# Local attention and FFN layers on one core: four hand-written orders of steps are replaced, and the next stage's first steps move among the last tiles

## The reference, cut to what matters

```python
for i in range(DEPTH):                               # DEPTH = 6
    x = attn_layer(shift_tokens(x), Wqkv[i], q_scale[i], k_scale[i], Wo[i]) + x
    x = ffn_layer(shift_tokens(x), ln_g[i], ln_b[i], W1[i], b1[i], W2[i], b2[i]) + x

# attn_layer: 16 heads of 64, window 32
q, k, v = jnp.split(x @ Wqkv, 3, -1)                 # 128 -> 3 x 1024
q = l2norm(q) * qs;  k = l2norm(k) * ksc             # then a rotary table on each
sim = q_window @ k_two_windows * 8, masked;  attn = softmax(sim, -1)
out = (attn @ v_two_windows) @ Wo
# ffn_layer: layer norm, 128 -> 2 x 341, a * gelu(gate), 341 -> 128
```

## Time and profile before

| what | value |
|---|---|
| runs | 2055.22, 2067.45, 2062.59 us, median 2062.59 |
| span of the profiled execution | 2060.2 us |
| PE busy | 1889.6 us, 92% of the span |
| DVE, ACT, POOL busy | 1444.6, 1395.0, 1448.5 us (70%, 68%, 70%) |
| mean granted TensorE clock | 0.967 |

### The profile page before, as it was taken

How to read it: one execution, slowest core, us unless ns; L and a number is a source line. 1 busy time by engine, 2 the same in 40 slices (tenths; PEclk the granted TensorE clock), 3 DMA queues, 4 the chain that set the end, 5 groups by cost and what they waited for, 6 DMA issues and landing times. The chain is left out here.

```text
span 2060.2 us, 77645 instructions
## 1 busy us (share of the span) xinstructions
PE 1889.6 (92%) x32069; PEld 1309.8 (64%) x32069; DVE 1444.6 (70%) x2609; ACT 1395.0 (68%) x2772; POOL 1448.5 (70%) x1839
## 2 busy tenths in 40 slices
PE   4648999999999999999999999999999999879959
PEld 3526666666666666666666666666666676656648
DVE  2357787678776877786778777877687778445546
ACT  1147877777777677877787778777777777534425
POOL 1158887787788778887888788878887888412334
PEclk9769999999999999999999999999999999979969
DMA  2012131111311111211113111121111111030012
GB/s 97 0 22 58 52 97 46 33 53 55 97 46 48 47 46 58 88 46 46 46 49 97 46 46 46 31 82 31 33 31 31 36 33 31 13 94 1 22 32 71
DMA packets 67087, 99.84 MB, mean 48 GB/s; under 512 B 15367, under 2 KB 51608, under 8 KB 65970
## 3 DMA queue, kind: packets, MB, share of 16 engines
q1 hardware_dynamic: 65234, 91.72, 15.4%
q0 software_dynamic: 1504, 3.17, 0.5%
HBM read 44.50 MB, written 21.45 MB: 32 GB/s over the span
## 5 line engine op out<-in xcount | busy, mean ns | idle before, releaser
L1284 PE MATMUL b_bank_proj<-layer_weights,b_stream_t 128*128 128x512 f32 x1152 | 587.1, 611 | 33.9 <-DVE b_plain_moved L1080 17.9
L1080 DVE TENSOR_TENSOR b_plain_moved<-b_bank_proj,b_rope 128x1024 f32<-128x1024 f32 x384 | 463.9, 1219 | 190.0 <-ACT b_squares L912 136.7
L820 POOL TENSOR_TENSOR b_rotated<-b_plain_moved 128x1024 f32<-128x1024 f32 x192 | 453.7, 2363 | 22.4 <-DVE b_plain_moved L1080 18.6
L835 POOL TENSOR_TENSOR b_rotated<-b_rotated,b_inv_norm 128x1024 f32<-128x1024 f32 x192 | 365.4, 1903 | 15.6
L943 ACT ACTIVATE b_k_t<-b_bank_shared 64x512 f32<-64x512 f32 x384 | 226.5, 590 | 121.9 <-PE b_bank_shared L1292 119.3
L912 ACT ACTIVATE b_squares<-b_bank_proj 128x512 f32<-128x512 f32 x384 | 229.2, 597 | 114.3 <-PE b_bank_proj L1284 109.9
L1284 PEld LDWEIGHTS b_bank_proj<-layer_weights,b_stream_t 128*128 128x128 f32 x1152 | 186.3, 191 | 135.9 <-issue 45.7
L840 POOL TENSOR_TENSOR b_probs<-b_probs,b_inv_sum 128x512 f32<-128x512 f32 x192 | 200.6, 1045 | 84.3 <-DVE b_inv_sum L1101 82.8
L1292 PE MATMUL b_bank_shared<-const_tables,b_rotated 128*128 128x128 f32 x1536 | 233.1, 277 | 17.4 <-POOL b_rotated L835 17.3
L934 ACT ACTIVATE b_q_t<-b_bank_shared 64x512 f32<-64x512 f32 x384 | 225.7, 588 | 34.3 <-PE b_bank_shared L1292 31.5
L1292 PEld LDWEIGHTS b_bank_shared<-const_tables,b_rotated 128*128 128x128 f32 x1536 | 177.9, 141 | 108.3 <-issue 92.5
(11 more groups left out here) (346 smaller groups left out, 2860.7 us busy)
## 6 DMA issues: line engine op xcount, KB each, us to landing
b_v_shifted<-b_v SPq DMA_DIRECT2D x96, 384.0 KB, 3.5
sorted_rows<-constants SPq DMA_DIRECT2D x135, 129.0 KB
layer_weights<-L_ffn_Wqkv SPq DMA_DIRECT2D x6, 1536.0 KB
b_v_shifted<-b_v SPq DMA_DIRECT2D x72, 128.0 KB, 3.4
layer_weights<-L_ffn_Wo SPq DMA_DIRECT2D x6, 512.0 KB
...
```

The lines of the kernel that those rows point to most:

```text
L820: nc.gpsimd.tensor_tensor(out=turned[:, k, :], in0=pm[:, k, 0, :], in1=pm[:, k, 1, :], op=ALU.add).then_inc(add_done, 1)
L835: nc.gpsimd.tensor_tensor(out=tk, in0=tk, in1=repeat_last(rn[:, k, :], DH), op=ALU.mult).then_inc(rope_done, 1)
L1080: nc.vector.tensor_tensor(to, src.to_broadcast(shape), tab.to_broadcast(shape), ALU.mult).then_inc(mul_done, 1)
L1284: nc.tensor.matmul(out, xs[:, b, t * P:(t + 1) * P], w, start=True, stop=True).then_inc(proj_full, 1)
```

## The change

Every engine's table is replaced by another one with the same steps, and `FIRST` names other places. No instruction is added or removed; the arithmetic is the same. The tables differ nearly everywhere, so of each only its first line stands here (the `- ` line is before):

```diff
 PE_TURN = [
-    ("scores", -1, 1), ("heads_t", 0, 1), ("project", 1, 0), ("project", 1, 1), ("pv", -2, 0), ("project", 1, 2),
+    ("leave", -3, 0), ("down", -2, 0), ("project", 1, 4), ("probs_t", -1, 0), ("enter", 2, 0), ("project", 1, 5),
...
 POOL_TURN = [
-    ("add", -2, 1), ("clamp", -2, 1), ("weigh", -4, 1), ("rstd", -2, 0), ("rope", -2, 1), ("clamp", -1, 0),
+    ("clamp", -8, 0), ("rope", -9, 1), ("add", -8, 0), ("weigh", -10, 0), ("weigh", -10, 1), ("rope", -8, 0),
...
 FIRST = {
-    "pe": {("scores", SLOTS - 1, 1): ("f_weights", "f_contexts"), ("probs_t", SLOTS - 1, 1): ("f_normed", "f_keys"),
-           ("pv", SLOTS - 1, 0): ("f_queries",), ("out", SLOTS - 1, 0): ("f_scores",), ("back", TURNS - 1, 0): ("leave", "f_counts")},
-    "act": {("attended", SLOTS - 2, 1): ("f_weights", "f_contexts"), ("probs_t", SLOTS - 1, 1): ("f_normed", "f_keys"),
-            ("attended", SLOTS - 1, 1): ("f_queries",), ("back", TURNS - 1, 0): ("f_scores", "leave", "f_counts")},
-    "dve": {("norms", SLOTS - 1, 1): ("f_stream",), ("share", SLOTS - 1, 1): ("f_normed",), ("residual", SLOTS - 2, 0): ("f_own",),
-            ("stats", TURNS - 1, 0): ("f_best",), ("scale", TURNS - 1, 0): ("f_counts",)},
-    "pool": {("rope", SLOTS - 1, 1): ("f_fill", "f_rstd")},
+    "pe": {("norm_t", TURNS - 1, 0): ("f_weights",), ("up", TURNS - 1, 2): ("f_contexts",), ("up", TURNS - 1, 3): ("f_normed",),
+            ("up", TURNS - 1, 5): ("f_keys", "f_queries",), ("down", TURNS - 1, 0): ("f_scores", "leave", "f_counts",)},
+    "act": {("gelu", TURNS - 1, 1): ("f_weights",),
+            ("gelu", TURNS - 1, 2): ("f_contexts", "f_normed", "f_keys", "f_queries", "f_scores", "leave", "f_counts",)},
+    "dve": {("residual", SLOTS - 3, 0): ("f_stream",), ("down", TURNS - 2, 0): ("f_normed",),
+            ("residual", SLOTS - 2, 0): ("f_own",), ("hidden", TURNS - 1, 2): ("f_best",), ("down", TURNS - 1, 0): ("f_counts",)},
+    "pool": {("add", SLOTS - 3, 0): ("f_fill",), ("weigh", SLOTS - 2, 1): ("f_rstd",)},
 }
```

More of the change, by code:

```diff
@@ new lines @@
+    ("heads_t", 1, 1), ("project", 2, 2), ("scores", 0, 1), ("pv", -1, 0), ("project", 2, 3), ("heads_t", 1, 2),
+    ("heads_t", 1, 3), ("out", -1, 0), ("project", 2, 4), ("project", 2, 5), ("back", -1, 0), ("heads_t", 2, 0),
+    ("project", 3, 0), ("probs_t", 0, 0), ("scores", 1, 0), ("scores", 1, 1), ("probs_t", 0, 1), ("heads_t", 2, 1),
+    ("project", 3, 1), ("pv", 0, 0), ("project", 3, 2), ("heads_t", 2, 2), ("heads_t", 2, 3), ("out", 0, 0),
+    ("norm_t", -1, 0), ("project", 3, 3), ("scores", 2, 0), ("up", -1, 0), ("probs_t", 1, 0), ("up", -1, 1),
@@ L504 @@
+    ("project", 5, 3), ("heads_t", 4, 2), ("heads_t", 4, 3),
 ]
 ACT_TURN = [
[L508 to L521, removed]
+    ("heads_t", -1, 2), ("heads_t", -1, 3), ("project", 0, 3), ("project", 0, 4), ("probs_t", -2, 0),
@@ new lines @@
+    ("project", 0, 5), ("root", 0, 1), ("project", 1, 0), ("probs_t", -2, 1), ("project", 1, 1), ("exp", -1, 0),
+    ("heads_t", 0, 0), ("heads_t", 0, 1), ("attended", -2, 0), ("project", 1, 2), ("attended", -2, 1),
+    ("project", 1, 3), ("exp", -1, 1), ("root", 1, 0), ("heads_t", 0, 2), ("heads_t", 0, 3), ("project", 1, 4),
+    ("project", 1, 5), ("probs_t", -1, 0), ("enter", 2, 0), ("project", 2, 0), ("leave", -3, 0), ("root", 1, 1),
+    ("project", 2, 1), ("probs_t", -1, 1), ("heads_t", 1, 0), ("heads_t", 1, 1), ("root", 2, 0), ("project", 2, 2),
@@ L522 @@
+    ("project", 3, 4), ("project", 3, 5), ("probs_t", 1, 1), ("project", 4, 0), ("root", 3, 1), ("project", 4, 1),
+    ("exp", 2, 0), ("attended", 1, 0), ("attended", 1, 1), ("project", 4, 2), ("heads_t", 3, 0), ("root", 4, 0),
+    ("exp", 2, 1), ("heads_t", 3, 1),
 ]
 DVE_TURN = [
-    ("residual", 0, 0), ("hidden", -1, 0), ("mul", 4, 0), ("norms", 4, 0), ("share", 2, 0), ("mul", 4, 1),
-    ("mul", 4, 2), ("soft", 2, 1), ("hidden", -1, 1), ("hidden", -1, 2), ("residual", 1, 0), ("share", 2, 1),
@@ L528 @@
[L528 to L532, removed]
```

34 lines of the change are left out of this document (24 added, 10 removed).

## The result

The changed kernel takes 2117.9 us (median of 4 runs, 2113.6 to 2120.0), the kernel before 2065.0 in the same series (2055.2 to 2067.5). The ratio is 1.0253, with a 95% interval from 1.0225 to 1.0281. The profiled spans, 2118.1 and 2060.2, differ by 57.9 us.

What follows compares the result with a forecast made beforehand. PE was taken as the bound, busy 66.38 of 67.31 us a turn. The profiled sum, 2060.2 - 22 (turns) - 11.5 (layer starts) + 2 (end of stage b) = 2028.7, gave a 2031 us median; range 2003 to 2062.

Steps and rivals of the forecast that it cites:

- term 2: PE's waits inside a turn of stage b: 1.3 us in place of 1.8, so 0.5 us a turn less.
- the floor of 64.9: PE's step times in a turn plus 0.1 us for each of 18 changes of pieces, without waits: 64.9 us.
- The sign that I had named for being wrong: Half-clock windows in mid-layer, or PE waiting on `b_attended_t` or `b_rotated` every turn, would show the forecast wrong; no size given.
- Term 1, the joints: PE's changes between small-matmul pieces and whole array: three pairs fewer, 0.5 us a turn less, bounds 0 and 0.6.
- rival (a): Small-matmul blocks side by side on PE save nothing: 2042 us, chance 0.13.
- rival (d): In the turns, `out` waits for ACT, its cover being 1.8 us: 2080 us, chance 0.12.
- Term 3, the layer starts: At five layer starts POOL's table ends 3 us earlier, sparing PE's wait: 11.5 us less, bounds 0 and 17 less.
- Term 4, the end of stage b: After the last `scores`, 5.0 us gained, but stage c's first steps now come last: +2 us, bounds -2 and +7.
- Term 5, the fill: In stage b's first 90 us PE waits for the first tiles whatever the order: 0, give or take 3 us.
- rival (c): All goes well: turns at the new table's floor plus 0.7 us, layer starts nearly free: 2009 us, chance 0.15.

Runs made afterwards that it cites:

- the kernel with 28 additions: Changed kernel with 28 repeated matmuls added in the first tile's `scores`, shifting the instruction borders by 112: 2076.9 us, ratio 1.0061.
- the version with two additions: Changed kernel with repeated matmuls added in `scores`, 29 in tile 0 and 48 in tile 48: 2047.5 us, ratio 0.9921.
- the one taken apart: Changed kernel with PE's table edited in three places, so projections separate `scores` and `pv` steps that stood side by side: 2066.8 us, ratio 1.0016.

## Why the prediction was wrong

**What failed** is a step of term 2: of the 67.31 us of a turn before it put 1.8 us down as "waits and gaps" over the floor of 65.5, and took 1.3 for the changed kernel, with 3.0 as the worst. The sum and the range rest on it. Measured, layer starts included, a turn of the changed kernel takes 1558.3 / 22 = 70.8 us, which is 5.9 over the floor of 64.9: of these 4.0 are stops for instructions (87.1 / 22) and 1.4 the low clock (30.7 / 22). The gaps were of another kind than waits for other engines, and they grew: stops rose by 94.2 - 16.9 = 77 us over the run. The trace of before had the rows (15 and 5 waits "for issue" in `pv` and `scores`); I took them for noise. The sign that I had named for being wrong, a low clock in the middle of a layer, did show (0.95 in the turn from 463.31).

**Term 1, the joints**, was right in kind. A pair of `scores` with no border in it takes 1.93 us from start to start in the kernel with 28 additions (x128 at 1349.55, the next step at 1351.48). Apart they take twice 1.03 and 0.14 to 0.19 for the second pair of changes, some 2.2. So a joint saves about 0.3, where I had 0.14 to 0.19, and rival (a), that it saves nothing, is out. I had asked what a joint saves on the array, and not what supplies it: two blocks side by side use 256 instructions in 1.9 us.

**Term 2, the waits in a turn**, was right and too small. Ordinary turns of the changed order less their stops are mostly 64.9 to 65.1 us in the version with two additions, those of before mostly 66.4 to 67.4: some 2 us a turn for terms 1 and 2 together, where I had 1.0. The floor of 64.9 was met. `heads_t` and `out` hardly wait (1.2 and 1.6 us in all), so rival (d), `out` waiting for ACT, didn't come in this kernel; it did in the one taken apart, with 13.6 us.

**Term 3, the layer starts**: DVE's wait for the table was to be half of the 36.0 of the earlier trace rows. In the list of waits:

```profile
DVE b_plain_moved L1079 <- POOL b_rope L806: 13.4, 5, 2.7
```

At the start of layer 2 PE's idle was 2.37 us, and is now 0.61, by the timeline:

```profile
696.49 1.12 PE L1283 MATMUL b_bank_proj<-layer_weights,b_stream_t 128*128 128x512 f32 x2 [0.61 <-DVE b_plain_moved L1079]
```

In the version with two additions the turn with that start takes 66.90 us, 0.4 more than the 66.48 of an ordinary one shown there, and the other two with a start and no addition or low clock 67.1 and 66.9, where I had left 1.5 of before's 4. The term holds.

**Term 4, the end of stage b.** From the last `scores` to the last copy of the stream it was 45.8 us. Of the changed kernel:

```profile
1823.64 1.99 PE L1310 MATMUL b_bank_scores<-b_k_t,b_q_t 128*32 128x64 f32 x128 [1.73 <-ACT b_k_t L942]
...
1873.96 0.60 DVE L1214 SCALAR_TENSOR_TENSOR layer_weights<-layer_weights 64x77 f32<-64x77 f32 x2
...
1875.99 0.60 ACT L982 ACTIVATE stream<-b_bank_shared 128x512 f32<-128x512 f32 x1 [2.92 <-PE b_bank_shared L1402]
```

From 1825.6 to 1876.6 that is 51.0, 5.2 more, of which 0.9 is a wait for issue ahead of `pv` at 1827.11; from `norm_t` of turn 22 to the end it is 2.1 more. I had +2, with -2 to +7. An order of steps with the old places was not run, so the term wasn't tried by itself. **Term 5, the fill**, came out at +4.7 where I had 0 with 3 either way; the stops up to `norm_t` of turn 0 sum to 7.4 us there, and to 2.6 before.

**The sum.** In the version with two additions, terms 1 to 3 show as 1721.06 - 242.70 = 1478.4 us from turn 0 to turn 22, by its `norm_t` rows, 28.9 less than before, with its own stops and the added work still in it. I had 33.5 less. In the changed kernel as it stands the rest of the table above is 47.0 less than before, so terms 1 to 3 together were too small rather than too large, and stops and clock add 74.2 and 23.9, which makes the 51.0 more. None of my rivals had it; (d) named its side, for a reason that didn't occur, and its worst case, 2099, lies under the 2117.9 measured. Two slips in the working change nothing: the steps as listed sum to 63.3 and not 63.1, and rival (c) leaves out the 2 us of term 4.
